# A Mamba mixer between two mixture-of-experts layers: dt's columns inside a unit of z, and that unit third in a block

## The reference

```
x = x + 0.5 * ffn(layernorm(x))
x = x + mixer(layernorm(x))
x = x + 0.5 * ffn(layernorm(x))

mixer(u):
  z, xBC, dt = split(u @ W_in.T, [1024, 1280, 16])      # 16 heads of 64, state 128
  xBC = silu(conv1d(xBC, taps=4, causal) + conv_b)
  x, B, C = split(xBC, [1024, 128, 128])
  dt = softplus(dt + dt_bias);  dA = exp(-dt * exp(A_log))
  state = dA * state + dt * x B^T;   y = state C + D * x
  y = y * silu(z)
  return (y * rsqrt(mean(y^2) + eps) * norm_w) @ W_out.T
```

## Time and profile before

| | us |
|---|---|
| median of 3 runs | 1483.61 (1481.75 to 1483.72) |
| the profiled execution | 1481.16 |
| its span in the profile | 1479.1 |
| PE busy | 1418.7 (96%) |
| DVE busy | 1052.5 (71%) |
| ACT busy | 784.7 (53%) |
| POOL busy | 794.9 (54%) |
| the mixer's four blocks begin at | 509.0, 622.65, 743.28, 862.45 |

### The profile page before, as it was taken

The page is one execution under the profiler, slowest core; times in us unless marked ns, Lnnn a source line. Parts: engine busy times, 40 slices in busy tenths (PEclk is TensorE's granted clock), DMA queues, the critical chain, the costliest instruction groups (busy, mean ns, idle before and its releaser), DMA issues. The chain is left out here.

```text
span 1479.1 us, 23406 instructions
## 1 busy us (share of the span) xinstructions
PE 1418.7 (96%) x8786; PEld 1217.8 (82%) x8786; DVE 1052.5 (71%) x1734; ACT 784.7 (53%) x1343; POOL 794.9 (54%) x496
## 2 busy tenths in 40 slices
PE   6999999999999999998999999889999999999999
PEld 5878999989987787787778779669779999999887
DVE  7584665567657798889879979967746656677466
ACT  4313666666632466576756656745025666666411
POOL 3103777777545344845743763752016776777533
PEclk9999999999999999999999999999999999999999
DMA  8232877777653220021012011016125777777435
GB/s 318 86 121 87 285 274 262 263 278 267 230 173 114 70 86 16 16 72 44 1 61 68 2 44 58 21 45 225 61 87 208 267 260 278 282 271 271 139 127 171
DMA packets 79743, 222.21 MB, mean 150 GB/s; under 512 B 8400, under 2 KB 16592, under 8 KB 78224
## 3 DMA queue, kind: packets, MB, share of 16 engines
q1 hardware_dynamic: 57552, 163.04, 31.4%
q0 software_dynamic: 11360, 37.23, 8.4%
q10 hardware_dynamic: 10720, 20.45, 3.9%
HBM read 183.47 MB, written 37.22 MB: 149 GB/s over the span
## 5 line engine op out<-in xcount | busy, mean ns | idle before, releaser
L666 POOL TENSOR_TENSOR g_lo<-g_raw,g_hi 128x1408 fp32r<-128x1408 f32 x54 | 180.5, 3343 | 113.9 <-ACT g_hi L834 111.6
L666 POOL TENSOR_TENSOR u_lo<-u_raw,u_hi 128x1408 fp32r<-128x1408 f32 x54 | 174.3, 3228 | 59.2 <-ACT u_hi L834 59.2
L1870 PE MATMUL bank<-u_hi,xgT 128*128 128x352 f32 x624 | 168.5, 333 | 0.0
L1893 PE MATMUL bank<-d_hi,hT 128*128 128x512 f32 (+1 forms) x468 | 159.4, 395 | 5.3 <-DVE hT L1174 5.3
L1870 PE MATMUL bank<-g_hi,xgT 128*128 128x352 f32 x624 | 163.0, 323 | 0.0
L696 POOL DMA_INDIRECT xg<-token_x,row_of x78 | 87.7, 1124 | 135.4 <-DVE row_of L1319 118.8
L884 ACT ACTIVATE gate<-bank 128x512 f32<-128x512 f32 (+1 forms) x48 | 28.7, 598 | 216.0 <-PE bank L1823 215.1
L752 POOL TENSOR_TENSOR w_hl<-w_raw,w_hl 128x1024 fp32r<-128x1024 f32 x35 | 88.3, 2523 | 91.6 <-ACT w_hl L834 91.6
L1838 PE MATMUL bank<-d_hi,hT 128*128 128x512 f32 (+1 forms) x384 | 128.5, 407 | 4.5 <-DVE hT L1174 2.4
L1174 DVE TENSOR_TENSOR d_lo<-d_raw,d_hi 96x512 fp32r<-96x512 f32 (+2 forms) x54 | 121.4, 2248 | 0.0
L1524 DVE SCALAR_TENSOR_TENSOR acc<-pre,cw,acc 128x512 f32<-128x512 f32 x120 | 114.8, 956 | 4.3
(11 more groups left out here) (264 smaller groups left out, 3570.2 us busy)
## 6 DMA issues: line engine op xcount, KB each, us to landing
g_raw<-in_w_gate SPq DMA_DIRECT2D x54, 704.0 KB, 6.0
u_raw<-in_w_up SPq DMA_DIRECT2D x54, 704.0 KB, 6.5
d_raw<-in_w_down SPq DMA_DIRECT2D x46, 512.0 KB, 5.0
w_raw<-in_w_in SPq DMA_DIRECT2D x36, 512.0 KB, 3.5
routed_y<-ys ACTq DMA_DIRECT2D x32, 512.0 KB, 4.7
d_raw<-in_w_down SPq DMA_DIRECT2D x46, 192.0 KB, 5.3
token_x<-xn SPq DMA_DIRECT2D x8, 1024.0 KB, 5.7
X<-in_x SPq DMA_DIRECT2D x4, 1024.0 KB, 10.6
```

The costliest lines, as they stand in the source:

```text
L666: pool.tensor_tensor(half_of(piece, 1, s), raw_at[piece][s % RING][:], half_of(piece, 0, s).bitcast(F), ALU.subtract)\
L1870: ins = pe.matmul(dst[:, 0:FE], xgT[:, n % 2, hx, kc], half_of(piece, hw, NS + j)[:, kc], start=(m == 0), stop=(m == 3 * KD - 1))
L1893: ins = pe.matmul(bank[Y + n % 2][:], hT[0:fw, hh, c, 0:P], half_of(2, hw, NS + j)[0:fw, c], start=(m == 0), stop=(m == 3 * NF - 1))
```

## The change

dt's 16 columns are appended to unit 5, which becomes 272 columns wide (`WD`); W_in's DRAM layout is padded to 272 columns for each unit, and the other units are loaded, split and used with 256 of them. In unit 5 each of the four tiles gets a bank of its own (6, 7, 4, 5), 256 columns of z and 16 of dt, and ScalarE evicts each with an instruction of its own. dt's own matmuls, its copy and its turning go away, and `softplus` reads the four banks with four adds. The order of units becomes 0, 1, 5, 2, 3, 4, 6, 7, 8. ScalarE's early `unit_hi(w + 2)` moves from unit 3 to unit 1, and the Exp between `softplus` and `log1p` from ahead of unit 5 to the end of unit 3. `pre` is placed where `L` lies. The waits follow: `m_res` and `m_yd`, till now waited for by dt's path, are waited for at `decay_sums` and in `sums_by_row`.

```diff
-ORDER = (0, 1, 2, 3, 5, 4, 6, 7, 8)
+WD = WU + HEADS
+DT_UNIT = 5
+DT_BANKS = (6, 7, 4, 5)
+ORDER = (0, 1, 5, 2, 3, 4, 6, 7, 8)
...
-    w_raw = mx("w_raw", [P, 2, KD, WU])
+    w_raw = mx("w_raw", [P, 2, KD, WD])
...
-    pre = mx_x("pre", [P, 2, TAPS - 1 + D])
+    pre = nc.alloc_sbuf_tensor_at("pre", [P, 2, TAPS - 1 + D], F, offset=L[:].tensor.manual_sbuf_range[0])
...
+    def width(u):
+
+        return WD if u == DT_UNIT else WU
...
-                    sp.dma_start(w_raw[:, w % 2], w_in[ORDER[w % NWU]]).then_inc(m_raw[w % 2], 16)
+                    wide = width(ORDER[w % NWU])
+                    sp.dma_start(w_raw[:, w % 2, :, 0:wide], w_in[ORDER[w % NWU], :, :, 0:wide]).then_inc(m_raw[w % 2], 16)
...
                     def conv_in(n, c):
 
                         b = bank[c % 2]
                         after(m_cp, n + 1, BPB * NCH)
+                        if c == 0:
+                            after(m_E, 2 * (n // NCH) * TB, 2 * TPB)
...
                         after(m_zp, j * 8 + (u - 5) * 2 + half + 1, 8 * BPB)
+                        if u == DT_UNIT:
+                            for q in (2 * half, 2 * half + 1):
+                                ins = act.activation(zs[:, q, 0:WU], bank[DT_BANKS[q]][:, 0:WU], ACT.Silu)
+                            ins.then_inc(m_z, 1)
+                            return
...
-                                    if (u, c) == (3, 7):
+                                    if (u, c) == (1, 3):
                                         unit_hi(w + 2)
...
-                                if u == 1:
-                                    after(m_dtT, j + 1, BPB)
-                                    after(m_yd, max(j * TB - 1, 0), TPB - 1)
-                                    act.activation(dtT, bank[3][0:HEADS, :], ACT.Copy).then_inc(m_dtc, 1)
-                            else:
-                                if u == 5:
+                                if u == 3:
                                     after(m_dx, j + 1, BPB)
                                     act.activation(d_e[:], d_z[:], ACT.Exp).then_inc(m_de, 1)
+                            else:
+                                if u == DT_UNIT:
...
-                            after(m_dtp, j + 1, BPB)
-                            own.step(dve.tensor_tensor(three(d_x), bank[2][:, 0:NQ].rearrange("p (q h) -> p q h", h=HEADS),
-                                                       some(hp[:, 0:HEADS], TB), ALU.add))
+                            after(m_zp, j * 8 + 2, 8 * BPB)
+                            for q in range(TB):
+                                own.mark(dve.tensor_tensor(d_x[:, q * HEADS:(q + 1) * HEADS], bank[DT_BANKS[q]][:, WU:WD],
+                                                           hp[:, 0:HEADS], ALU.add))
+                            own.join()
...
                             after(m_csT, j + 1, BPB)
+                            after(m_yd, max(j * TB - 1, 0), TPB - 1)
...
                             after(m_ap, j + 1, BPB)
+                            after(m_res, j * TB, TPB)
...
-                                if u == 1:
-
-                                    pe.wait_ge(m_wdt_lo, 1)
-                                    for m, (kc, (hw, hx)) in enumerate([(c, h) for c in range(KD) for h in HALVES]):
-                                        ins = pe.matmul(bank[3][0:HEADS, :], wdt[:, hw, kc], xb[:, hx, kc],
-                                                        start=(m == 0), stop=(m == 3 * KD - 1))
-                                    ins.then_inc(m_dtT, 1)
-                                if u == 2:
-                                    after(m_dtc, j + 1, BPB)
-                                    after(m_res, j * TB, TPB)
-                                    for q in range(TB):
-                                        ins = pe.matmul(bank[2][:, q * HEADS:(q + 1) * HEADS], dtT[:, q * P:(q + 1) * P],
-                                                        ident[0:HEADS, 0:HEADS], start=True, stop=True)
-                                    ins.then_inc(m_dtp, 1)
...
-                                    if u == 5:
+                                    if u == DT_UNIT and half == 0:
                                         wait_residual(pe, k)
                                         after(m_ylo, 2 * j * TB, 2 * TPB)
                                         after(m_yi, 2 * j * TB, 2 * TPB)
+                                    elif u == DT_UNIT:
+                                        after(m_S, j * TB, TPB - 1)
+                                        after(m_xD, j * TB, TPB)
                                     else:
                                         after(m_z, n - 1, 8 * BPB)
+                                        after(m_dx, j + 1, BPB)
...
+                                        dst = bank[DT_BANKS[q]][:, 0:WD] if u == DT_UNIT else \
+                                            bank[place][:, (q % 2) * WU:(q % 2 + 1) * WU]
```

More of the change, by code:

```diff
@@ L114, in step, with program @@
         self.join()
-def program(nc, x, w_router, w_gate, w_up, w_down, w_down_shared, w_in, w_dt, conv, heads, norm_w, w_out, out):
+def program(nc, x, w_router, w_gate, w_up, w_down, w_down_shared, w_in, conv, heads, norm_w, w_out, out):
     token_x = nc.dram_tensor("token_x", (TOK, D), mybir.dt.float32, kind="Internal").ap()
@@ L262, in program @@
     xg = nc.alloc_sbuf_tensor_at("xg", [P, XG, D], F, offset=xn_at)
[L263 to L264 removed]
+    yg01 = nc.alloc_sbuf_tensor_at("yg01", [P, 2, TOPK, D], F, offset=xn_at + 2 * KD * WD * 4)
+    yg23 = nc.alloc_sbuf_tensor_at("yg23", [P, 2, TOPK, D], F, offset=xn_at + 2 * KD * WD * 4 + 6 * D * 4)
     yg = [yg01[:, 0], yg01[:, 1], yg23[:, 0], yg23[:, 1]]
@@ L311, in program @@
     mx_x = placer(xs1_at)
-    w_hl = mx_x("w_hl", [P, 2, 2, KD, WU], R)
-    pre = mx_x("pre", [P, 2, TAPS - 1 + D])
+    w_hl = mx_x("w_hl", [P, 2, 2, KD, WD], R)
+    pre = nc.alloc_sbuf_tensor_at("pre", [P, 2, TAPS - 1 + D], F, offset=L[:].tensor.manual_sbuf_range[0])
     place_of = lambda t: t[:].tensor.manual_sbuf_range
@@ L320, in program @@
     assert place_of(acc)[0] >= place_of(yg01)[1] and place_of(xgT)[1] <= xs1_at
-    assert place_of(acc)[1] <= place_of(yg23)[0] and place_of(yg23)[1] <= place_of(wdt_raw)[0]
-    assert place_of(wdt_raw)[0] >= xn_at + 3 * TB * D * 4 and place_of(cs_rows)[1] <= xs0_at
+    assert place_of(acc)[1] <= place_of(yg23)[0] and place_of(yg23)[1] <= place_of(halo)[0]
+    assert place_of(halo)[0] >= xn_at + 3 * TB * D * 4 and place_of(cs_rows)[1] <= xs0_at
     assert place_of(g_lo[0])[1] <= place_of(zs)[0] + 2 * DI * 4 and place_of(u_lo[0])[1] <= place_of(zs)[0] + 3 * DI * 4
-    assert place_of(w_hl) == place_of(xs1)
+    assert place_of(w_hl)[0] == place_of(xs1)[0] and place_of(pre)[1] <= place_of(L)[1]
     bank = [nc.alloc_psum_tensor(f"bank{i}", [P, 512], F) for i in range(8)]
@@ L605, in mixer @@
                 for j in range(2):
-                    sp.dma_start(w_raw[:, j], w_in[j]).then_inc(m_raw[j], 16)
-                sp.dma_start(wdt_raw[:], w_dt).then_inc(m_wdt, 16)
+                    sp.dma_start(w_raw[:, j, :, 0:WU], w_in[j, :, :, 0:WU]).then_inc(m_raw[j], 16)
                 for w in range(2, NB * NWU):
                     sp.wait_ge(m_wlo, w - 1)
-                    sp.dma_start(w_raw[:, w % 2], w_in[ORDER[w % NWU]]).then_inc(m_raw[w % 2], 16)
+                    wide = width(ORDER[w % NWU])
+                    sp.dma_start(w_raw[:, w % 2, :, 0:wide], w_in[ORDER[w % NWU], :, :, 0:wide]).then_inc(m_raw[w % 2], 16)
             for k, what in enumerate(PLAN):
@@ L731, in mixer @@
                 pool.wait_ge(m_whi, 1)
-                pool.tensor_tensor(w_hl[:, 0, 1], w_raw[:, 0], w_hl[:, 0, 0].bitcast(F), ALU.subtract).then_inc(m_wlo, 1)
+                pool.tensor_tensor(w_hl[:, 0, 1, :, 0:WU], w_raw[:, 0, :, 0:WU], w_hl[:, 0, 0, :, 0:WU].bitcast(F),
+                                   ALU.subtract).then_inc(m_wlo, 1)
                 for piece in range(2):
@@ L751, in unit_lo @@
                         after(m_whi, w + 1, BPB * NWU)
-                        pool.tensor_tensor(w_hl[:, w % 2, 1], w_raw[:, w % 2], w_hl[:, w % 2, 0].bitcast(F),
-                                           ALU.subtract).then_inc(m_wlo, 1)
+                        cols = slice(0, width(ORDER[w % NWU]))
+                        pool.tensor_tensor(w_hl[:, w % 2, 1, :, cols], w_raw[:, w % 2, :, cols],
+                                           w_hl[:, w % 2, 0, :, cols].bitcast(F), ALU.subtract).then_inc(m_wlo, 1)
                     def rms(n):
@@ L994, in mixer @@
                 act.wait_ge(m_raw[0], 16)
-                split_hi(w_hl[:, 0, 0], w_raw[:, 0], m_whi)
+                split_hi(w_hl[:, 0, 0, :, 0:WU], w_raw[:, 0, :, 0:WU], m_whi)
                 for piece in range(4):
@@ L1008, in unit_hi @@
                             after(m_zp, jj * 8 + (u - 5) * 2 + 2, 8 * BPB)
-                        split_hi(w_hl[:, w % 2, 0], w_raw[:, w % 2], m_whi)
```

(10 more changed lines are left out.)

18 lines of the change are left out of this document (removed).

## The result

The kernel after takes 1490.07 us (median of 20 runs, 1485.83 to 1497.35) against 1485.67 (20 runs, 1480.21 to 1492.06) beside it: ratio 1.0029, 95% interval 1.0015 to 1.0042, a loss of 4.3 us (2.2 to 6.2). A second measurement gave 1491.07 against 1485.44, 1.0029 again (1.0012 to 1.0046).

The account below looks back on a forecast made before the run. VectorE's chain and TensorE together bound the stretch to `products`. Lateness, softplus and fewer stalls sum to +6.9 us: 1481.16 profiled gives 1488.1, plus 2.45 to the median, 1490.5; range +3 to +12, 1486.6 to 1495.6.

Parts of the forecast that it names:

- VectorE and TensorE arrive together: At `products` in block 1, VectorE and ScalarE finish the last channel at 681.6, TensorE starts at 681.83; shortening one gains nothing.
- Channel 4 late by 3.28 us: The widened z unit (6.07 us) replaces dt (2.79) ahead of channel 4, so VectorE's chain to `products` starts 3.28 us late.
- halves with a row gap in SBUF: Weight halves in SBUF: taken as before; 0.2 us more of GpSimd for each would add 1 us per block.
- TensorE's relief: Per block, dt's matmuls and transposes leave TensorE (-3.78 us), wider matmuls add 0.32: -3.46 us.
- Five stalls become four, 9.7 us becomes 8.3: VectorE after channel 4, held by GpSimd's subtractions: position 4's falls in idle time, four remain at 2.0 to 2.2 us each.
- the rule of the Trainium skill: GpSimd and VectorE instructions using a second SBUF port or two SBUF inputs lock each other out for a whole instruction.
- rival (c): GpSimd's subtraction for position 4 comes late enough to meet channel 4: 2.1 us more per block, 1498.9 us; chance 0.12.
- rival (b): One more subtraction falls where VectorE waits or reads PSUM: -2.1 us per block, 1482.1 us, no measurable change; chance 0.16.
- The block's sum: First unit to `products`: lateness, softplus and stalls give +2.1 us in blocks 1 and 3, +1.3 in 2, +1.4 in 0.
- TensorE's waits of 3.8, 0.9, 0.5 and 0.2: TensorE before `products`: waits at position 6, for `aparts`, `cs_rows` and the last channel, 5.4 us of new idle time.
- The loads, `softplus` and `pre`: Loads in 1 KB runs land in 4 us, nothing on the path; softplus +0.2 us per block; `pre` costs nothing.
- The sum: Whole kernel: +6.9 us over four blocks, stated as 1490.5 us; chance 0.60.

Follow-up runs that it names:

- the kernel without the wait: The kernel after, with ScalarE's half for position 6 made early, inside unit 3 ahead of Exp: 1506.08 us, ratio 1.0134 to before.
- the pair with less work on GpSimd: Kernels before and after, GpSimd's subtraction cut to the first of four kc after the buffers' first uses: 1475.03 us without dt's folding, 1466.15 with it.
- short DMA runs: The kernel before with W_in padded to 272 columns in DRAM, so loads go in 1 KB runs: 1485.44 us, ratio 1.0016.
- TensorE kept busy: The kernel after, with 24 unused matmuls (2.9 us) ahead of position 6: 1496.64 us, ratio 1.0064 to before; run again, 1492.42 us, 1.0059.
- the order alone: The kernel before with the new order of units (unit 5 third), dt keeping its own matmuls: 1502.19 us, ratio 1.0123.
- the old order: The kernel after with unit 5 back in fifth place, softplus behind channel 7, Exp behind unit 5's evictions: 1493.43 us, ratio 1.0052 to before.
- unit 5 fourth: The kernel after with order 0, 1, 2, 5, 3, 4, 6, 7, 8 and ScalarE's early half at channel 5: 1489.85 us, ratio 1.0015 to before.

## Why the prediction was right

**VectorE and TensorE arrive together; shortening TensorE gains nothing.** Shown by two experiments together: in the kernel without the wait TensorE came early to the next gate and stood there for 6.3 us, and in the pair with less work on GpSimd the same fold takes 8.4 us off the stretches.

**Channel 4 late by 3.28 us.** Measured from the block's first unit it is 28.34 us in place of 24.38: 3.96. The widened unit takes 6.16 start to start in place of 6.07, and the place of dt is reached 0.55 us later than before. Part of that (0.2 us, two units of the convolution) is a cost that I had set at nothing, probably that of halves with a row gap in SBUF. A unit of the convolution takes 5.67 us start to start in after (624.29 to 629.96) and in every kernel whose `w_hl` has rows of 272, against 5.58 in before and in the kernels with rows of 256, that with short DMA runs among them; no run varies the row gap by itself. TensorE's relief is therefore nearer to 3.0 than to 3.46 us per block; the busy times of the pair with less work on GpSimd differ by 3.05.

**Five stalls become four, 9.7 us becomes 8.3.** Four there are, of 2.0, 2.0, 2.15 and 1.5 = 7.7 us. The fourth met not the taps of channel 8 but the casts behind them, because position 6 took longer: with TensorE kept busy it meets the taps (675.34, 4.35 us), and the four come to the 8.3 us forecast. So the low clock also saved VectorE some 0.5 us. The cast at 677.99, which reads PSUM, again takes 0.41 us beside a subtraction, and the one at 678.89 is held. By the rule of the Trainium skill that the prediction weighs (SBUF — State Buffer, section "SBUF: two separate sides"), the trace agrees. The price of 1.22 us for the same subtraction on VectorE itself speaks for a lock by GpSimd's instruction and against its traffic. The subtraction for position 4 ends as channel 4 begins, so rival (c) was as near as could be, and rival (b) did not come.

**The block's sum.** In block 1: 3.96 late, 2.0 less stalls, 0.2 for four adds in place of one, and 0.2 more from the last Silu to `products` come to +2.4, as measured; +2.1 was forecast. The last 0.2 are TensorE's: its rows have no gap from 668.99 to 685.90, and the last Silu had ended at 685.41. Blocks 0, 2 and 3 were forecast at +1.4, +1.3 and +2.1 and came at +2.95, +1.88 and +3.66 (+3.12, +1.89 and +2.21 in the second profile). Block 0 is short in the profile of before: in the kernel with short runs, where the first block begins as early as in after, it takes 55.94 us, and against that it is +1.8. In block 3 the slow unit took 8.67 us in one profile and 7.23 in the other, which is the whole difference of 1.45: there TensorE at the low clock set the end, and that is not in the prediction. The mechanism holds, with this addition.

**TensorE's waits of 3.8, 0.9, 0.5 and 0.2.** The first came (3.68 to 3.82). The others did not, for a reason that the prediction lacks: the clock fell to half behind the first and TensorE spent the later waits on a slow unit. With TensorE kept busy the other three are 0.77, 0.25 and, where the profile shows it, 0.17. The low clock ate time in which TensorE would have waited anyway, and so it cost only some 1.5 us over the four stretches (0.3 to 2.7 from profile to profile).

**The loads, `softplus` and `pre`.** As forecast: 4.0 us, 0.41 us for four adds, no new wait.

**The sum.** +6.9 was forecast; 8.4 came between two profiles, but 4.4 between the medians (ratio: 4.3, 2.2 to 6.2), so the change in the time was overstated by some 2.5 us. The base of the forecast was the median of three runs, 2 us below that of twenty. The two misses cancel, and that 1490.07 lies so close to 1490.5 is luck. The stretches grew by 10.9 and 9.6 us in the two profiles, more than the 6.9. The clock (some 1.5 of it), the early start of block 0 (1.1) and channel 4's being 0.7 later in the block than forecast are the causes that the traces show; they overlap and were not parted further.

## What to carry to other kernels

When two engines arrive at a gate together, taking work from one pays only after the other's chain is shorter: here the same edit cost 4 us, and took 8 off the stretches once VectorE had slack. Read what lengthens the other chain before moving work ahead of its input; here an instruction of GpSimd that held VectorE for 2.0 us was cheaper on VectorE itself, at 1.2. A unit moved ahead of the first link of a chain delays the chain by its length (here by 3.96 us, net of dt's matmuls that left), and only the stalls that vanish with it give some back.

## What the hardware showed unexpectedly

TensorE's granted clock fell from 1.00 to 0.50 behind waits of 3.68 us (after), 6.33 (the early half), 2.62 (the order alone), 2.49 (the old order) and 1.87 (unit 5 fourth, block 2), and the unit behind took 6.9 to 8.7 us in place of 5.9; behind waits of 0.87 and 1.28 it stayed at 1.00. But it also stayed at 1.00 behind 2.00 (the old order, block 2) and 2.81 (the order alone, block 2), so the length of the wait alone doesn't decide. Timeline of the kernel with the order alone, blocks 1 and 2:

```profile
674.12 7.49 PE L2140 MATMUL bank<-w_hl,xs 128*128 128x256 f32 x48 [2.62 <-POOL w_hl L752]
...
799.42 6.01 PE L2140 MATMUL bank<-w_hl,xs 128*128 128x256 f32 x48 [2.81 <-POOL w_hl L752]
```

Matmuls with stationary weights from rows of 272 fp32 ran 24 in 5.67 us, against 5.58 from rows of 256, in kernels that differ in more than the rows. And the first stage, the same code in all these kernels, ended between 508 and 516 us, with the clock between 40 and 80 us at 0.96 in the earliest and 0.87 in the latest; for one kernel both came up.
